# The last self-attention of a fused Perceiver kernel: V held in TensorE, the result not turned, one exponential per head, weighing a step later, division on POOL

## The chip, the cores and the metric

The kernel runs on one core of a Trainium2 chip, as one launch. The metric is device time in microseconds of a whole launch, from several runs. The trace shown is of one more execution, taken by the hardware profiler.

## What is computed

Two layers over 128 batches of 32 tokens of width 256 (`x`), each layer a cross-attention to 257 context rows, a self-attention and a feed-forward part. Only the last self-attention and what follows it are touched:

```python
x = x + _L1_attn_ref(_layernorm(x, axis=-1), L1_attn_W_qkv, L1_attn_W_out)
x = x + _L1_ffn_ref(_layernorm(x, axis=-1), L1_ffn_weight)

def _L1_attn_ref(x, W_qkv, W_out):        # 16 heads of 64, sequences of 32
    qkv = jnp.einsum('bse,ef->bsf', x, W_qkv)
    q, k, v = (qkv[:, :, 0], qkv[:, :, 1], qkv[:, :, 2])
    q = rotary_embedding(q, seq_len, HEAD_DIM)
    k = rotary_embedding(k, seq_len, HEAD_DIM)
    scores = jnp.einsum('bqhd,bkhd->bhqk', q, k) * scale
    scores = jnp.where(mask, scores, NEG_INF)          # causal
    weights = jax.nn.softmax(scores, axis=-1)
    out = jnp.einsum('bhqk,bkhd->bqhd', weights, v)
    return jnp.einsum('bsf,fe->bse', out, W_out)
```

`_L1_ffn_ref` is a BitLinear: a product with weights rounded to -1, 0, 1 and inputs rounded to 8 bits.

## The kernel before

The program runs stage after stage; the last, `SelfAttention1`, begins near 1975 us. It works in groups of 128 rows (4 batches of 32 tokens, `BPG` = 4), 32 groups. Work is pipelined over steps by hand: every engine's program walks through `steps()`, and in step g it does its share for group g (projections, rotation), for g - 1 (softmax), g - 2 (output projection) and, nine steps later, for the BitLinear. Engines wait for each other by named semaphores. What an engine does is in the order in which its function writes it.

In step g, TensorE (`tensor`) does: `project` of q and k in halves of 512 columns (each 6 matmuls, since every product is made of a high and a low part), between them `turn_out`, which turns the weighed and divided result of group g - 2 by eight transposes (L2243); `turn` of q's rotated halves (eight transposes, L2230); the `scores` of group g - 1 (L1161); v's first half; k's first turned half; `project_out` of g - 2 (24 matmuls); in one step of four, the next four groups' normalised input is turned (`ln.turn`, L353); k's second turned half; v's second half; the BitLinear's `turn` (L2122); `weigh` of group g - 1 (L1210); the BitLinear's `product` (L2139). Matrices in f32 of the scores and the weighing are recorded twice in the trace: 64 matmuls in the program are 128 there, and 32 are 64.

Results of the projections, of the turns, of the output projection and of the BitLinear share four PSUM banks (`Ring`): each use takes the next bank, and waits for the engine that emptied it four uses before. The scores lie in two banks of their own and the weighed result (`ps_out`) in two others.

VectorE (`vector`) forms the rotation's two products per half (`rotate`, L2365, L2368), the low part of the turned result (`attn_lo`, L2377), then the softmax of g - 1: mask and scale (L1181), maximum (L1186), shift (L1188), and, when ACT's one exponential of 512 columns (L1167) is done, the transpose in blocks of 32 (L1194), the sums (L1195) and their inverse (L1201); the addition of the output projection to X (L2403); statistics and rounding for other groups; the product of the weighed result with the inverse (L2424); the BitLinear's addition (L2146). POOL adds the rotation's two products (L2439) in two buffers `rot`, each of which it may overwrite when TensorE has turned it. ACT copies q, k (`keep_turned`, L2316), v (`keep_v`, L2309) and the high part of the turned result (`attn_hi`, L2323).

The weighing, which the change turns round, is

```python
ins = pe.do.matmul(out[rows, h, :], probT[rows, c0:c0 + T], v[rows, h * dv:(h + 1) * dv], start=True, stop=True)
```

with the turned probabilities (32 x 32) as the operand that is loaded and v (32 x 64) as the one that is streamed.

## Time and profile before

| | us |
|---|---|
| median of 3 runs | 2576.3 |
| lowest, highest | 2574.9, 2583.25 |
| the profiled execution | 2582.01 |
| its span, first to last instruction | 2580.1 |
| TensorE's mean granted clock in it | 0.964 of full |
| busy in the span: TensorE, its loads, VectorE, ACT, POOL | 2406.9, 1981.7, 1812.8, 1253.8, 841.0 |

A row of a timeline has the start, the duration, the engine, the line and the operation with its shape; several equal instructions in a row are merged, with their number behind x. Neighbours on an engine overlap, so what one costs is read from start to start. Rows of groups give the number, the total busy time and the mean duration in ns of one. Rows of windows give, for a stretch, its length, each engine's busy time with the number of instructions, TensorE's granted clock, and what the DMA engines did.

### The profile page before, as it was taken

The page shows a single profiled execution, that of the slowest core. Times are in us where ns is not written, and L with a number is a line of the kernel's source. Part 1 is how long each engine was busy: PE and PEld are TensorE (multiplying, and loading weights), DVE is VectorE, ACT ScalarE, POOL GpSimd, SP SyncE. Part 2 cuts the span into 40 slices and gives each one's busy share as a digit, 9 for nine tenths or more (in the row PEclk, how much of TensorE's full clock was granted, in tenths as well). Part 3 has the DMA queues.
Part 4 walks back from the last instruction along what each step waited for, and adds up shares of the span by engine and source line. Part 5 has one row for each costly group of instructions (what it writes and reads, how often), then busy time and mean ns, then how long its engine had stood idle before and what let it go on. Part 6 is the DMA issues. An engine that isn't in the chain of part 4 may idle for free. (4 is left out here: it accounts for less than half of the span.)

```text
span 2580.1 us, 103373 instructions
## 1 busy us (share of the span) xinstructions
PE 2406.9 (93%) x44640; PEld 1981.7 (77%) x44640; DVE 1812.8 (70%) x3820; ACT 1253.8 (49%) x2826; POOL 841.0 (33%) x740
## 2 busy tenths in 40 slices
PE   7999999999988867999996999999997999999997
PEld 6888888888855545888885777777776888888885
DVE  6778777777756664222225888888886788888886
ACT  5666666666544423333334777777763223232332
POOL 3333333332222112433335444444221333333231
PEclk9999999999998867999998999999997999999998
DMA  6555555554323244111115888887772000000000
GB/s 204 147 147 158 157 156 151 156 156 125 101 58 101 77 162 178 48 52 46 49 43 167 237 232 235 234 236 224 221 203 86 3 3 3 11 11 11 11 11 26
DMA packets 199554, 298.98 MB, mean 116 GB/s; under 512 B 29368, under 2 KB 107324, under 8 KB 197824
## 3 DMA queue, kind: packets, MB, share of 16 engines
q1 hardware_dynamic: 192288, 275.58, 36.1%
q0 software_dynamic: 6816, 16.79, 2.0%
q8 instruction: 356, 5.83, 1.0%
q14 instruction: 94, 0.77, 0.1%
HBM read 170.75 MB, written 78.77 MB: 97 GB/s over the span
## 5 line engine op out<-in xcount | busy, mean ns | idle before, releaser
L839 ACT ACTIVATE prob_x<-ps_score_x,neg_max_x 128x257 f32<-128x257 f32 x1024 | 403.6, 480 | 203.4 <-DVE neg_max_x L907 203.4
L907 DVE TENSOR_REDUCE neg_max_x<-ps_score_x 128x2 f32<-128x514 f32 x512 | 329.0, 684 | 108.2 <-PE ps_score_x L723 107.0
L734 PEld LDWEIGHTS ps_v_x<-v_wide_x,probT_x 128*32 128x32 f32 x18432 | 288.4, 108 | 126.8 <-issue 121.4
L734 PE MATMUL ps_v_x<-v_wide_x,probT_x 128*32 128x68 f32 x18432 | 336.0, 223 | 25.0 <-issue 20.2
L931 DVE STREAM_TRANSPOSE probT_x<-prob_x 128x1152 f32<-128x1152 f32 x256 | 344.0, 1344 | 0.0
L1073 POOL TENSOR_TENSOR ctxT_x_lo<-ready,ctxT_x_hi 128x514 fp32r<-128x514 f32 x128 | 153.0, 1196 | 386.5 <-ACT ctxT_x_hi L818 304.9
L2439 POOL TENSOR_TENSOR rot_s<-turned_s,swapped_s 128x512 f32<-128x512 f32 x128 | 164.5, 1297 | 327.7 <-DVE swapped_s L2368 288.1
L1073 POOL TENSOR_TENSOR split<-loaded,split 128x514 fp32r<-128x514 f32 x128 | 153.7, 1201 | 326.8 <-ACT split L818 302.2
L230 PE MATMUL ps_x<-split,w_q_x_hi 128*128 128x258 f32 x1024 | 208.0, 300 | 10.3 <-POOL split L1073 8.6
L1979 DVE TENSOR_TENSOR hid_moe<-ps_up_moe,silu_moe 128x512 f32<-128x512 f32 x71 | 49.1, 692 | 202.9 <-PE ps_up_moe L230 202.9
L723 PE MATMUL ps_score_x<-kT_x,q_x 32*64 32x257 f32 x4096 | 177.7, 401 | 14.3 <-ACT prob_x L839 10.3
L230 PEld LDWEIGHTS ps_x<-split,w_q_x_hi 128*128 128x128 f32 x1024 | 159.9, 192 | 31.0 <-issue 16.2
L830 ACT ACTIVATE kT_x<-ps_x,bias_k 128x257 f32<-128x257 f32 x256 | 122.2, 478 | 126.1 <-PE ps_x L230 125.6
L923 DVE STREAM_TRANSPOSE v_x<-ps_x 128x288 f32<-128x288 f32 x256 | 121.4, 480 | 74.3 <-PE ps_x L230 73.9
L230 PE MATMUL ps_x<-ctxT_x_hi,w_v_x_hi 128*128 128x258 f32 x512 | 159.0, 311 | 10.5 <-POOL ctxT_x_lo L1073 10.5
L230 PE MATMUL ps_x<-ctxT_x_hi,w_k_x_hi 128*128 128x258 f32 x512 | 146.4, 286 | 6.3 <-DVE v_x L923 6.3
L2323 ACT ACTIVATE attnT_s_hi<-ps_s 128x512 fp32r<-128x512 f32 x64 | 38.1, 599 | 231.4 <-PE ps_s L2243 231.4
L230 PE MATMUL ps_x<-split,w_q_x_lo 128*128 128x258 f32 x512 | 146.4, 286 | 0.5 <-issue 0.5
L230 PE MATMUL ps_x<-ctxT_x_lo,w_v_x_hi 128*128 128x258 f32 x512 | 145.0, 283 | 0.0
L230 PE MATMUL ps_x<-ctxT_x_hi,w_v_x_lo 128*128 128x258 f32 x512 | 144.9, 283 | 0.0
L230 PE MATMUL ps_x<-ctxT_x_lo,w_k_x_hi 128*128 128x258 f32 x512 | 144.9, 283 | 0.0
L230 PE MATMUL ps_x<-ctxT_x_hi,w_k_x_lo 128*128 128x258 f32 x512 | 144.4, 282 | 0.0
(296 smaller groups left out, 6010.0 us busy)
## 6 DMA issues: line engine op xcount, KB each, us to landing
v_wide_x<-v_x SPq DMA_DIRECT2D x512, 76.5 KB, 2.2
v_out_x<-v_x SPq DMA_DIRECT2D x128, 306.0 KB, 4.3
v_wide_x<-v_out_x SPq DMA_DIRECT2D x512, 76.5 KB, 3.1
ready<-ctx SPq DMA_DIRECT2D x128, 257.0 KB, 3.6
loaded<-ctx SPq DMA_DIRECT2D x128, 257.0 KB, 4.2
gate_whole<-moe_experts SPq DMA_DIRECT2D x32, 256.0 KB, 3.7
lo_out<-gate_whole SPq DMA_DIRECT2D x32, 256.0 KB
w_moe<-lo_out SPq DMA_DIRECT2D x8, 1024.0 KB, 8.3
```

The source lines that it names most:

```text
L230: last = pe.do.matmul(out, a, b, start=n == 0, stop=n == len(steps) - 1)
L723: ins = pe.do.matmul(self.ps[m * 2 * T:(m + 1) * 2 * T, r, 0:S], q, self.kT[b % 3][rows, m, 0:S], start=True, stop=True)
L734: ins = pe.do.matmul(self.ps_v[r * T:(r + 1) * T, b % 2, :, :], self.probT[b % 3][:, r, n * T:(n + 1) * T], self.v_wide[b % 4][:, :, r, n, ...
L830: act.do.activation(out, src, ACT.Identity, bias=self.biases["k"][:, m:m + 1]).then_inc(*s.k.at(tag, b, m))
L839: act.do.activation(self.prob[b % 3][:, r, 0:S], self.ps[:, r, 0:S], ACT.Exp, bias=self.neg_max[b % 2][:, r:r + 1]).then_inc(*s.exp.at(tag ...
L907: dve.do.tensor_reduce(self.neg_max[b % 2][:, r], self.ps[:, r, 0:S], AX_X, ALU.max, negate=True).then_inc(*s.neg_max.at(tag, b, half))
L923: dve.do.transpose(out.rearrange("p x n d -> p n x d"), src.rearrange("p (n x d) -> p n x d", x=2, d=XD)).then_inc(*s.v.at(tag, b, m))
L931: dve.do.transpose(flat(self.probT[b % 3]), flat(self.prob[b % 3])).then_inc(*s.prob_T.at(tag, b))
L1073: pool.do.tensor_tensor(self.ctxT[b % 3].lo[:, :, 0:S], self.ctx_in[g % 2][:, j, :, :], self.ctxT[b % 3].hi[:, :, 0:S].bitcast(F32), ALU.s ...
L1979: dve.do.tensor_tensor(self.hid[t % 2][:, :], self.up_ps[t % 2][:, :], self.silu[t % 2][:, :], ALU.mult).then_inc(*s.hid.at(t))
L2323: act.do.activation(self.attnT.hi[:, c * 512:(c + 1) * 512], banks["attn", g, c][:, :], ACT.Copy).then_inc(*s.a_hi.at(g, c))
L2439: pool.do.tensor_tensor(self.rot[e][:, :, :], self.turned[e][:, :, :], self.swapped[e][:, :, :], ALU.add).then_inc(*s.r_rot.at(g, i, c))
```

## The change

- The scores stand first in TensorE's step, and the weighing is that of group g - 2, behind the four half products of q and k. Scores and result now share four banks (`ps_halves`): scores in the first 256 columns of two, the result in the other 256 of all four. So the scores wait for the last use of the result (`a_lo`), and the weighing waits until VectorE has masked the new scores.
- In the weighing v is the operand that is loaded and the turned probabilities are streamed. The result then lies as the output projection needs it; `turn_out`, the tile `attn` and the semaphore `a_T` go.
- ACT takes one exponential per head, 16 of 32 columns, each with its maximum as bias and its sum as a second result. VectorE's shift and sums go. The inverse (`divide`) stays there.
- The probabilities are divided before they are weighed: POOL multiplies them with the inverse (`even`), behind its four rotation additions, and VectorE turns them after that. VectorE's product of the result with the inverse goes.
- On VectorE mask and maximum stand first in the step, the turn behind the other groups' statistics and rounding and ahead of the addition to X.

```diff
     def exponent(self, act, g):
+        s, t, e = self.s, self.t, g % 2
+        act.wait_ge(s.s_max, "s1", g)
         if g >= 2:
+            act.wait_ge(s.s_probT, "s1", g - 2)
+            act.wait_ge(s.s_inv, "s1", g - 2)
+        for n in range(H):
+            own = slice(n * T, (n + 1) * T)
+            ins = act.do.activation(t["prob"][e][:, own], t["shifted"][e][:, own], ACT.Exp, bias=t["neg_max"][e][:, n:n + 1],
+                                    accum_out=t["sums"][e][:, n:n + 1])
+        ins.then_inc(*s.s_exp.at("s1", g))
...
+    def even(self, pool, g):
+        s, t, e = self.s, self.t, g % 2
+        by_head = lambda a: a.rearrange("p (h q) -> p h q", q=T)
+        pool.wait_ge(s.s_inv, "s1", g)
+        pool.do.tensor_tensor(by_head(t["prob"][e][:, :]), by_head(t["prob"][e][:, :]),
+                              t["inv"][e][:, :].unsqueeze(2).to_broadcast([P, H, T]), ALU.mult).then_inc(*s.s_even.at(g))
+
+    def turn(self, dve, g):
+        s, t, e = self.s, self.t, g % 2
+        dve.wait_ge(s.s_even, g)
         if g >= 2:
-            dve.wait_ge(s.s_pv, tag, g - 2)
-        dve.do.transpose(t["probT"][e][:, :], t["prob"][e][:, :]).then_inc(*s.s_probT.at(tag, g))
...
+            dve.wait_ge(s.s_pv, "s1", g - 2)
+        dve.do.transpose(t["probT"][e][:, :], t["prob"][e][:, :]).then_inc(*s.s_probT.at("s1", g))
...
     def weigh(self, pe, g, out, v, dv):
-        s, tag, probT = self.s, self.tag, self.t["probT"][g % 2]
-        pe.wait_ge(s.s_probT, tag, g)
-        for h in range(H):
-            c0 = self.order.column[h]
-            for b in range(BPG):
-                rows = slice(b * T, (b + 1) * T)
-                ins = pe.do.matmul(out[rows, h, :], probT[rows, c0:c0 + T], v[rows, h * dv:(h + 1) * dv], start=True, stop=True)
-        ins.then_inc(*s.s_pv.at(tag, g))
+        s, probT = self.s, self.t["probT"][g % 2]
+        pe.wait_ge(s.s_probT, "s1", g)
+        for n in range(H // 2):
+            for x in range(2):
+                h = 2 * n + x
+                c0 = self.order.column[h]
+                for b in range(BPG):
+                    rows = slice(b * T, (b + 1) * T)
+                    ins = pe.do.matmul(out[x * dv:(x + 1) * dv, b, n, :], v[rows, h * dv:(h + 1) * dv], probT[rows, c0:c0 + T],
+                                       start=True, stop=True)
+        ins.then_inc(*s.s_pv.at("s1", g))
...
+    def out_part(self, c):
+
+        return self.out[:, 2 * c:2 * c + 2, :, :]
+
+    def attn_part(self, t, c):
+
+        return t[:, :].rearrange("p (n b q) -> p b n q", n=H // 2, q=T)[:, 2 * c:2 * c + 2, :, :]
```

TensorE's order within a step:

```diff
+            if before:
+                pe.wait_ge(s.r_qkT, g - 1, 1, self.NB - 1)
+                if g >= 3:
+                    pe.wait_ge(s.a_lo, g - 3, 0)
+                self.soft.scores(pe, g - 1, q_k)
             if now:
                 project(g, 0, 0)
                 project(g, 0, 1)
-            if out:
-                turn_out(g - 2, 0)
-            if now:
                 project(g, 1, 0)
                 project(g, 1, 1)
             if out:
-                turn_out(g - 2, 1)
+                pe.wait_ge(s.s_v, tag, g - 2, self.NB - 1)
+                if before:
+                    pe.wait_ge(s.s_masked, g - 1)
+                self.soft.weigh(pe, g - 2, self.out, self.v[g % 2], D1)
             if now:
+                project(g, 2, 0)
                 turn(g, 0, 0)
                 turn(g, 0, 1)
-            if before:
-                pe.wait_ge(s.r_qkT, g - 1, 1, self.NB - 1)
-                self.soft.scores(pe, g - 1, q_k)
-            if now:
-                project(g, 2, 0)
-                turn(g, 1, 0)
             if out:
                 project_out(g - 2)
+            if now:
+                turn(g, 1, 0)
             if n < SG and j == 3:
                 for k in range(KD):
                     self.ln.turn(pe, n, k, banks)
             if now:
                 turn(g, 1, 1)
-                project(g, 2, 1)
             if 0 <= last < G:
                 self.bit.turn(pe, last)
-            if before:
...
+            if now:
+                project(g, 2, 1)
             if 0 <= last < G:
                 self.bit.product(pe, last)
```

ACT's:

```diff
+            if before:
+                self.soft.exponent(act, g - 1)
             if out:
+                attn_hi(g - 2, 1)
                 attn_hi(g - 2, 0)
-                attn_hi(g - 2, 1)
             if now:
+                keep_v(g, 0)
                 keep_turned(g, 0, 0)
                 keep_turned(g, 0, 1)
```

VectorE's, and at the end POOL's:

```diff
+            if before:
+                self.soft.mask(dve, g - 1)
             if now:
                 rotate(g, 0, 0)
                 rotate(g, 0, 1)
             if g == 0:
                 self.wqkv[2].split_lo(dve)
-            if out:
-                attn_lo(g - 2, 0)
             if now:
                 rotate(g, 1, 0)
                 rotate(g, 1, 1)
+            if before:
+                self.soft.divide(dve, g - 1)
             if out:
                 attn_lo(g - 2, 1)
+                attn_lo(g - 2, 0)
+            if n < SG and j == 1:
+                for i in range(GPS):
+                    self.ln.take_stats(dve, n, i)
+            if n < SG and j == 2:
+                self.ln.scale(dve, n)
+            if 0 <= done < SG:
+                if jd == 1:
+                    self.bit.quantise(dve, done)
+                if jd == 2:
+                    self.bit.round_z(dve, done)
             if before:
-                self.soft.softmax(dve, g - 1)
+                self.soft.turn(dve, g - 1)
             if out:
                 dve.wait_ge(s.a_o_ps, g - 2)
                 dve.do.tensor_tensor(self.X[:, g - 2, :], self.X[:, g - 2, :], banks["o", g - 2][:, 0:D], ALU.add).then_inc(
                     *s.s_x1.at(g - 2))
             if n < SG and j == 3:
                 prepare(n)
-            if n < SG and j == 1:
-                for i in range(GPS):
-                    self.ln.take_stats(dve, n, i)
-            if n < SG and j == 2:
-                self.ln.scale(dve, n)
             if 0 <= g - 3 < G:
                 self.bit.take_stats(dve, g - 3)
-            if 0 <= done < SG:
-                if jd == 1:
-                    self.bit.quantise(dve, done)
-                if jd == 2:
-                    self.bit.round_z(dve, done)
-            if before:
-                dve.wait_ge(s.s_pv, tag, g - 1)
-                dve.wait_ge(s.s_inv, tag, g - 1)
-                if g >= 2:
-                    dve.wait_ge(s.a_T, g - 2, self.NB - 1)
-                dve.do.tensor_tensor(self.attn[:, :].rearrange("p (h d) -> p h d", d=D1), self.out,
-                                     self.t["inv"][(g - 1) % 2][:, :].unsqueeze(2).to_broadcast([P, H, D1]), ALU.mult).then_inc(
-                    *s.s_out.at(tag, g - 1))
...
+            if before:
+                self.soft.even(pool, g - 1)
```

What stands where is shown at two places. VectorE, the softmax and what follows it in one step before (`prob_s` are the probabilities, `X` the running sum):

```order
L1181 SCALAR_TENSOR_TENSOR shifted_s<-ps_score_s,constants 128x256 x2
L1186 TENSOR_REDUCE neg_max_s<-shifted_s 128x16
L1188 TENSOR_TENSOR shifted_s<-shifted_s,neg_max_s 128x512
L1194 STREAM_TRANSPOSE probT_s<-prob_s 128x512
L1195 TENSOR_REDUCE sums_s<-prob_s 128x16
L1201 RECIPROCAL inv_s<-sums_s 128x2x8
L2403 TENSOR_TENSOR X<-X,ps_s 128x256
```

And in the change, from the inverse to the next group's maximum, in a step that also rounds for the BitLinear:

```order
L1188 RECIPROCAL inv_s<-sums_s 128x16
L2375 TENSOR_TENSOR attnT_s_lo<-ps_halves_s,attnT_s_hi 128x2x8x32 x2
L2113 TENSOR_SCALAR xn_bit<-xn_bit,inv_bit 128x256 x4
L2116 TENSOR_SCALAR xn_bit<-xn_bit 128x1024
L2118 TENSOR_SCALAR xn_bit<-xn_bit 128x1024
L1202 STREAM_TRANSPOSE probT_s<-prob_s 128x512
L2414 TENSOR_TENSOR X<-X,ps_s 128x256
L2076 BN_STATS stats_bit<-X 128x6
L2078 BN_AGGR mv_bit<-stats_bit 128x2
L2150 SCALAR_TENSOR_TENSOR X<-ps_s,back_bit,X 128x256
L1166 SCALAR_TENSOR_TENSOR shifted_s<-ps_halves_s,constants 128x256 x2
L1170 TENSOR_REDUCE neg_max_s<-shifted_s 128x16
```

The transpose of the probabilities, which followed the shift at once, now stands behind the other groups' rounding and directly ahead of the addition to X; the mask and the maximum of the next group end the row, at the head of the next step.

POOL in the last stage had only the rotation's additions, with a root now and then. In the change, around two steps (`rot_s` are the rotated halves, `rstd` and `var` the norms' statistics):

```order
L1194 TENSOR_TENSOR prob_s<-prob_s,inv_s 128x512
L2432 TENSOR_TENSOR rot_s<-turned_s,swapped_s 128x512 x4
L1194 TENSOR_TENSOR prob_s<-prob_s,inv_s 128x512
L321 TENSOR_TENSOR ln_rstd_s<-ln_var_s,constants 128x4
L2432 TENSOR_TENSOR rot_s<-turned_s,swapped_s 128x512 x4
```

The division (L1194) of a group stands behind all four additions of the step.

## Rows read from the trace of the kernel before

**Rows 1.** Busy time by stretch: the last stage's opening, and its steady part

```profile
1975.00:1999.00 24.00, 21.59 (x332) 17.32 (x331) 15.01 (x34) 8.25 (x13) 8.06 (x7) 0.81 0.01 2
2141.00:2529.00 388.00, 384.66 (x7304) 334.50 (x7303) 322.26 (x703) 117.05 (x223) 120.32 (x97) 1.00 0.03 9
```

**Rows 2.** Timeline of TensorE, step 2: the scores of group 1

```profile
2006.47 1.29 PE L1161 MATMUL ps_score_s<-loaded 64*32 64x32 f32 x128
```

**Rows 3.** Timeline of TensorE, one whole step, 2501.84 to 2521.60 us

```profile
2501.84 1.99 PE L1210 MATMUL ps_out_s<-loaded,probT_s 32*32 32x64 f32 x128
2503.76 0.39 PE L2139 MATMUL ps_s<-wq_bit,zT_bit 128*128 128x256 bf16 x2
2503.91 0.71 PE L230 MATMUL ps_s<-split,xT_s_hi 128*128 128x512 f32 x2
...
2506.75 0.60 PE L2243 MATMUL ps_s<-constants,attn_s 128*128 128x128 f32 x4
2507.10 0.48 PE L230 MATMUL ps_s<-w_qkv_s_hi,xT_s_hi 128*128 128x512 f32 x1
...
2509.98 0.60 PE L2243 MATMUL ps_s<-constants,attn_s 128*128 128x128 f32 x4
2510.42 1.04 PE L2230 MATMUL ps_s<-constants,rot_s 128*128 128x128 f32 x8
2511.39 1.29 PE L1161 MATMUL ps_score_s<-loaded 64*32 64x32 f32 x128
2512.60 0.50 PE L230 MATMUL ps_s<-w_qkv_s_hi,xT_s_hi 128*128 128x512 f32 x1
...
2514.11 0.60 PE L2230 MATMUL ps_s<-constants,rot_s 128*128 128x128 f32 x4
2514.46 0.36 PE L230 MATMUL ps_s<-w_out_s_hi,attnT_s_hi 128*128 128x256 f32 x1
...
2517.39 0.60 PE L2230 MATMUL ps_s<-constants,rot_s 128*128 128x128 f32 x4
...
2521.60 0.71 PE L230 MATMUL ps_s<-split,xT_s_hi 128*128 128x512 f32 x2
```

**Rows 4.** TensorE, first self-attention's scores and what follows; loads of two forms (min/median/max ns)

```profile
868.90 0.86 PE L1332 MATMUL ps_score_s<-kT_s,q_s 32*64 32x32 f32 x64
869.69 0.55 PE L353 MATMUL ps_s<-constants,ln_xn_moe 128*128 128x128 f32 x3
...
L1332 PEld LDWEIGHTS ps_score_s<-kT_s,q_s x2048: 127/131/227, 743.1 to 934.3; 32*64 32x64 f32 x187
...
L1210 PEld LDWEIGHTS ps_out_s<-loaded,probT_s x4096: 101/105/105, 1996.4 to 2548.5; 32*32 32x32 f32 x196
```

**Rows 5.** Groups of POOL, whole program

```profile
L2439 POOL TENSOR_TENSOR rot_s<-turned_s,swapped_s 128x512 f32<-128x512 f32 x128 | 164.5, 1297 | 327.7 <-DVE swapped_s L2368 288.1 <-PE ps_s L2230 37.7
...
L1082 POOL TENSOR_TENSOR loaded<-loaded,share_routed 128x1024 f32<-128x1024 f32 x14 | 26.5, 1895 | 0.0
```

**Rows 6.** Groups of VectorE, last stage; and its timeline, the shift

```profile
L2377 DVE TENSOR_TENSOR attnT_s_lo<-ps_s,attnT_s_hi 128x512 fp32r<-128x512 f32 x64 | 43.4, 681 | 2.1 <-ACT attnT_s_hi L2323 2.1
...
L1194 DVE STREAM_TRANSPOSE probT_s<-prob_s 128x512 f32<-128x512 f32 x32 | 22.8, 713 | 22.3 <-ACT prob_s L1167 22.3
...
L2403 DVE TENSOR_TENSOR X<-X,ps_s 128x256 f32<-128x256 f32 x32 | 13.4, 419 | 19.0 <-PE ps_s L230 19.0
...
2514.23 0.69 DVE L1188 TENSOR_TENSOR shifted_s<-shifted_s,neg_max_s 128x512 f32<-128x512 f32 x1
```

**Rows 7.** Groups of ACT, whole program; and its timeline, four exponentials

```profile
L839 ACT ACTIVATE prob_x<-ps_score_x,neg_max_x 128x257 f32<-128x257 f32 x1024 | 403.6, 480 | 203.4 <-DVE neg_max_x L907 203.4
...
L1167 ACT ACTIVATE prob_s<-shifted_s 128x512 f32<-128x512 f32 x32 | 20.2, 632 | 92.4 <-DVE shifted_s L1188 92.4
...
L1448 ACT ACTIVATE prob_moe<-logit_moe 128x32 f32<-128x32 f32 x8 | 1.8, 229 | 10.4 <-DVE logit_moe L1456 10.3
...
1502.86 1.58 ACT L839 ACTIVATE prob_x<-ps_score_x,neg_max_x 128x257 f32<-128x257 f32 x4 [0.99 <-DVE neg_max_x L907]
```

110 lines of the change are left out of this document (36 added, 74 removed).

## The prediction

> **What bounds the kernel now.** Read the busy time by stretch first [rows 1]: in the steady part of the last stage TensorE is busy for 384.66 of 388.00 us at the full clock (1.00, the 2.4 GHz level), while VectorE has 83% (322.26 of 388), ACT 30%, POOL 31%. So what TensorE issues is the bound there; only the opening (21.59 busy of 24) and the tail are bound by chains. Then one step in order of time [rows 3], from 2503.91 to 2521.60: 17.69 us. Each piece's cost is the distance to the next piece's start, since the durations overlap. The scores of group 1 start at 2006.47 [rows 2] and those of group 29 at 2511.39 [rows 3], 28 steps of 18.03 us on average, so this one is 0.34 under the mean. Everything before 1975 us is the same program before and after.
>
> **The change, part by part.** Steps are counted from the moment at which TensorE starts a piece [rows 3].
>
> (1) The eight transposes of the weighed result (L2243) go: 2507.10 - 2506.75 = 0.35 and 2510.42 - 2509.98 = 0.44 us.
>
> (2) The weighing takes 2503.76 - 2501.84 = 1.92 us for 128 recorded matmuls, 15.0 ns each, with 32 columns loaded and 64 streamed. It becomes 64 loaded and 32 streamed. The trace has exactly that form in the first self-attention's scores (32*64, 32x32) [rows 4]: 64 of them in 869.69 - 868.90 = 0.79 us, 12.3 ns each, so 128 x 12.3 = 1.58 us, 0.34 less. The ends: the pace of the last self-attention's own scores, 2512.60 - 2511.39 = 1.21 us for 128, and no gain at all, 1.92. I take 1.58, the row of the same form. The Trainium skill ("TensorE: Matmul & The Clock Gate", section on LDWEIGHTS) says that a load's time goes with its columns; by that the new order, with twice the columns to load, would be slower, not faster. The rows of the loads agree in kind, 131 ns against 105 [rows 4], but the pace of the pair is what TensorE pays, and that is lower in the row. The rule has a rival below.
>
> (3) The rest of TensorE's step is moved, not changed. With the starts of rows 3 I lay it out anew, in us from the start of the scores: scores 0 (1.21 long), q's and k's four half products 1.21 to 6.96 (1.51 + 1.44 after the scores, 2.80 for the next two, which no longer follow transposes), weighing 6.96 to 8.54, v's first half to 10.05 (1.51), q's eight transposes to 10.85 (0.35 + 0.45), output projection to 13.78 (2.93 = 2517.39 - 2514.46), k's eight transposes to 14.58, then 0.31 for the BitLinear's two, v's second half from 14.89 to 16.37 and the BitLinear's product to 16.52 (0.15 = 2503.91 - 2503.76; the 0.31 and 1.48 are what is left of 2521.60 - 2517.39 without 0.36 for four transposes, 1.92 and 0.15, shared as two transposes and six matmuls go elsewhere in the step). So 17.69 - 16.52 = **1.17 us less per step**, if nothing makes TensorE wait.
>
> (4) POOL's division is a new link. POOL has only two rotation buffers, so its third addition waits until TensorE has turned the first: that was at once done before, and is now behind the weighing. q's first transposes start at 10.05 and end at 10.65 (0.60 long [rows 3]). Then two additions (1.30 long [rows 5], and I take 1.25 from one to the next) put the division at 13.19. What does it cost? An addition of 512 columns on POOL took 1.30, a product with a broadcast operand of 1024 columns 1.90 [rows 5]; half of the latter is 0.95. I take 1.30, the row of the same size; the ends are 0.95 and 1.90. It ends at 14.49. VectorE, held there, then turns the probabilities (0.71 long) and adds to X (0.42) [rows 6], the second starting 0.08 before the first ends, as neighbours on VectorE do: 14.53, 15.16, 15.58. v's second half takes the bank that this addition to X empties (four banks in a ring: output, k's two, the BitLinear's turn, v) and would start at 14.89. So **TensorE waits 15.62 - 14.89 = 0.73 us** in each step that has a BitLinear turn in it (from step 9 on). The three or four tasks that stand ahead of the turn on VectorE end earlier in most steps. The earlier steps have no such turn; there v's second half takes another bank, and the wait is absent.
>
> (5) Sixteen exponentials per group instead of one. Their length: 480 ns for 257 columns with a bias from memory, four in 1.58 us, so 367 ns apart; one column costs (632 - 229) / 480 = 0.84 ns [rows 7]. For 32 columns that is 291 ns long and 178 apart: 16 x 0.178 = 2.9 us. No row shows an activation that also writes its sum. If the sum is free it is 2.9 us; if each sum is an instruction of its own as long as the 32-column activation (229 ns) and nothing overlaps, 16 x (291 + 229) = 8.3 us. They start where the shift started, 2514.23 - 2511.39 = 2.84 after the scores' start [rows 3, 6]. ACT then makes two copies of the weighed result (0.63 each at most, by the 512-column activation [rows 7]) and VectorE two subtractions (0.68 each [rows 6]) behind them, each of these 0.04 to 0.08 less from start to start: the copies can start at 8.65, when the weighing's last result is out, the last subtraction is ready at some 10.6, and the output projection wants it at 10.85. From 2.84 to 8.65 are 5.8 us, and 0.2 more are slack, so there is room for 6.0 us of exponentials before anyone waits. The middle of the two ends, 5.6, is still hidden, so I put this at nothing. The cover is ACT's idle time, 70% of the stretch [rows 1]; were it gone, the 5.6 would show in every step.
>
> (6) VectorE loses the shift (0.69 [rows 6]), the sums and the product with the inverse; at 83% it isn't the bound, so this buys only room. Reading the result in four banks and writing it in runs of 32 I put at the old rows' durations.
>
> (7) **Opening and tail.** In the opening the weighing of group 0 (1.92) leaves its step, and some of the 2.41 us idle [rows 1] can be filled: 3 us less, ends 0 and 5. The tail, 2580.1 - 2521.60 = 58.5 us now, loses the transposes and gains the exponentials and the division in its two chains: 1 us less, ends -6 and +4.
>
> The sum: eight early steps 8 x 1.17 = 9.4; 21 late ones 21 x (1.17 - 0.73) = 9.2; the mean of a step is 0.34 above 17.69, over 29 steps 10 us, most of it the normalised groups' transposes, which stay; of its gaps I let 2.1 go, ends 0 and 4; opening and tail 4. Together 24.7. The profiled execution took 2582.0 us (span 2580.1) and would take 2557.3; the median of the runs is 5.7 us lower, 2576.3, so I forecast **2551 us**.
>
> **The rivals.**
>
> A. The sums hold up ACT. At 8.3 us the exponentials end 2.3 us past the 6.0 that are free. The output projection starts that much later, the 0.73 is swallowed by it, and a late step takes 16.52 + 2.3 = 18.8 against 17.69, an early one as much more than now. That is 1.1 in 29 steps, 32 us, and some 5 in the tail, less 3 of the opening: 2610 us, slower. It decides from 6.0 + 1.17 = 7.2 us of exponentials, 450 ns each. For: no row shows the form. Against: it needs no overlap at all, where neighbours overlap by 113 ns each [rows 7]. The Trainium skill ("VectorE: DVE Perf Modes", section on two Vector instructions with no wait between them) says that an operation that writes its accumulator out is two instructions; if ACT does the same, this rival is how it would hurt. No row here shows it.
>
> B. The division is slow on POOL, 1.9 us. Then the wait is 1.33, a late step saves nothing (-0.16), and what is left is 9.4 + 2.1 + 4 - 3.4 = 12: 2564 us.
>
> C. Loading bounds the weighing. Then it goes with the loads' rows, 1.92 x 131 / 105 = 2.40 us, 0.82 more than my term in 31 groups, 25 us: 2576 us, no change. Against it stands the pace of the same form [rows 4].
>
> D. Better than forecast: weighing at the scores' pace, 1.21 (0.37 x 31 = 11), and a division of 1.05 (0.25 x 21 = 5): 2535 us.
>
> **How the numbers follow.** Forecast 0.50, A 0.10, B 0.15, C 0.06, D 0.19. The predicted time is the forecast's. The range runs from just below D (the opening's end too) to above B: 2532 to 2572 us; outside lie A, most of C and the lower part of D. A measurement can tell 0.3% (7.7 us) from no change. Faster: forecast, B and D less a little of B that ends near 2569, 0.82. Same: C and that part, 0.08. Slower: A, 0.10.
>
> **What would show it.** In the changed profile: no L2243 transposes; the weighing (ps_halves) at about 1.6 us from start to start; a late step of some 17.2 us between scores; TensorE idle before v's second half, released by VectorE's addition to X, 0.7 us per step; POOL's division near 1.3 us, waiting for nothing on POOL itself but standing behind two additions that waited for TensorE's transposes; the exponentials of a group within 6 us. It is wrong if a late step takes 17.7 or more, if the output projection waits for the rest of the result (A), if the weighing's pace is above 15 ns (C), or if the step is 16.6 with no wait at all (then the link in (4) isn't there).

## The result and the profile after

The changed kernel takes **2592.03 us** (median of 10 runs, 2584.77 to 2599.34) against 2582.06 for the kernel before (median of 10, 2574.9 to 2587.06; the 2576.3 of the start was the median of its first three, so 5.8 us of what my forecast missed lie in its starting point). The ratio is 1.0032, 95% interval 1.002 to 1.0043: slower, by a little more than the 0.3% that I said a measurement can tell. I forecast 2551 us. The profiled execution took 2592.01 us (span 2590.2), against 2582.01 (2580.1) before.

Busy time by stretch, after; the rows answer to [rows 1] (columns: stretch, its length, busy us and instructions of TensorE, its loads, VectorE, ACT and POOL, granted clock, DMA share, GB/s).

```profile
1975.00:1999.00 24.00, 18.19 (x205) 13.93 (x206) 15.80 (x36) 12.63 (x45) 8.99 (x8) 0.93 0.01 2
2141.00:2529.00 388.00, 359.15 (x7087) 301.75 (x7086) 305.66 (x621) 205.04 (x858) 138.91 (x114) 0.98 0.03 9
```

TensorE was busy for 384.66 of the 388 us before and is for 359.15 now, at a clock of 0.98: it has less to do, and waits. VectorE is busy for 305.66 us where it was for 322.26, though the change took away three of its instructions in every step.

One late step on TensorE, from one group's scores to the next, answers to [rows 3]: 2471.03 to 2490.59, 19.56 us.

```profile
2471.03 1.29 PE L1157 MATMUL ps_halves_s<-loaded 64*32 64x32 f32 x128
...
2478.02 1.49 PE L1213 MATMUL ps_halves_s<-probT_s,loaded 32*64 32x32 f32 x128
2479.44 0.50 PE L230 MATMUL ps_s<-w_qkv_s_hi,xT_s_hi 128*128 128x512 f32 x1
...
2480.94 1.03 PE L2240 MATMUL ps_s<-constants,rot_s 128*128 128x128 f32 x8
...
2484.66 1.03 PE L2240 MATMUL ps_s<-constants,rot_s 128*128 128x128 f32 x8
2485.53 0.38 PE L2126 MATMUL ps_s<-constants,xn_bit 128*128 128x128 f32 x2
2487.95 0.50 PE L230 MATMUL ps_s<-w_qkv_s_hi,xT_s_hi 128*128 128x512 f32 x1 [2.04 <-DVE X L2414]
...
2490.01 0.65 PE L2143 MATMUL ps_s<-wq_bit,zT_bit 128*128 128x256 bf16 x2
```

Up to 2485.53 the step is shorter than I laid it out (the BitLinear's turn starts 14.50 us in; I had 14.58). Then v's second half waits for VectorE's addition to X: the view shows 2.04 us of idle time, and it starts 16.92 us in, where I had 15.62 after a wait of 0.73. The waits of TensorE in the steady stretch, in sum (us, times, longest):

```profile
PE ps_s L230 <- DVE X L2414: 15.9, 16, 2.1
PE ps_s L2240 <- DVE X L2414: 11.2, 5, 2.2
```

The second row is the same wait in the five steps that also turn the layer norm's input: there k's second turned half takes the bank that the addition to X empties.

What holds VectorE is in the timelines of VectorE and POOL of the same step:

```profile
2480.24 1.29 DVE L2375 TENSOR_TENSOR attnT_s_lo<-ps_halves_s,attnT_s_hi 128x512 fp32r<-128x512 f32 x2 [0.52 <-ACT attnT_s_hi L2322]
2481.45 4.06 DVE L2113 TENSOR_SCALAR xn_bit<-xn_bit,inv_bit 128x256 f32<-128x256 f32 x4
2485.55 0.69 DVE L2116 TENSOR_SCALAR xn_bit<-xn_bit 128x1024 f32<-128x1024 f32 x1
2486.27 0.69 DVE L2118 TENSOR_SCALAR xn_bit<-xn_bit 128x1024 f32<-128x1024 f32 x1
2486.88 0.71 DVE L1202 STREAM_TRANSPOSE probT_s<-prob_s 128x512 f32<-128x512 f32 x1
2487.51 0.38 DVE L2414 TENSOR_TENSOR X<-X,ps_s 128x256 f32<-128x256 f32 x1
```

```profile
2475.43 2.68 POOL L2432 TENSOR_TENSOR rot_s<-turned_s,swapped_s 128x512 f32<-128x512 f32 x2 [9.82 <-DVE swapped_s L2367]
2481.71 2.59 POOL L2432 TENSOR_TENSOR rot_s<-turned_s,swapped_s 128x512 f32<-128x512 f32 x2 [3.60 <-PE ps_s L2240]
2484.26 1.10 POOL L1194 TENSOR_TENSOR prob_s<-prob_s,inv_s 128x512 f32<-128x512 f32 x1
```

Four TENSOR_SCALARs of 256 columns take 4.06 us. They start 0.26 before POOL's two additions and its division, and end 0.15 after them; the first of 1024 columns, next to no POOL instruction, takes its usual 0.69. Taken one by one, the first of the four takes 0.345 us and the others end at 2483.155, 2484.452 and 2485.511, each 0.15 behind the end of a POOL instruction (2483.004, 2484.300, 2485.360). Lengths over the stage (min/median/max ns), after and then before:

```profile
L2097 DVE TENSOR_SCALAR xn_bit<-X,mv_bit,rstd_bit x24: 403/1256/1391, 2091.8 to 2464.6; 128x256 f32<-128x256 f32 x24
L2113 DVE TENSOR_SCALAR xn_bit<-xn_bit,inv_bit x24: 343/1258/1454, 2112.2 to 2484.4; 128x256 f32<-128x256 f32 x24
L333 DVE TENSOR_SCALAR ln_xn_s<-X,ln_mean_var_s,ln_rstd_s x28: 404/1256/1394, 2010.5 to 2447.3; 128x256 f32<-128x256 f32 x28
```

```profile
L2093 DVE TENSOR_SCALAR xn_bit<-X,mv_bit,rstd_bit x24: 382/407/412, 2103.2 to 2467.2; 128x256 f32<-128x256 f32 x24
L2109 DVE TENSOR_SCALAR xn_bit<-xn_bit,inv_bit x24: 321/347/350, 2120.3 to 2483.8; 128x256 f32<-128x256 f32 x24
```

So three of every four are held up, in all three tasks: the BitLinear's quantising (L2097) and rounding (L2113) and the layer norm's scaling (L333). They do not cost the same. Late steps without a task take 17.1 to 17.5 us; those that round 18.7 to 20.2; those that quantise 19.7 to 21.3, of which some 1.6 are the layer norm's transposes that fall into the same step (18.03 against 16.44 in run 4 below). A late step that only scales takes 17.3, or 18.3 where TensorE also waits 0.85 ahead of the scores, as it does in run 4. Its four end at 2448.49, 0.15 behind POOL's division, and the turn that waits for the division follows at once (VectorE's timeline):

```profile
2444.42 4.07 DVE L333 TENSOR_SCALAR ln_xn_s<-X,ln_mean_var_s,ln_rstd_s 128x256 f32<-128x256 f32 x4
2448.41 0.70 DVE L1202 STREAM_TRANSPOSE probT_s<-prob_s 128x512 f32<-128x512 f32 x1
```

Behind the rounding's four stand two passes of 0.69, behind the quantising's a maximum of 1.22 and three short instructions; these are what the held-up task pushes past the division. Early steps take 16.0 us, with the scaling or with no task (17.36 before).

For the experiments one measure is used beside the time: the start of group 29's scores less that of group 1's, 28 steps, as for [rows 2, 3]. Before: 2511.39 - 2006.47 = 504.92. Seven of the 28 are early and 21 late, so by my terms it should have come to 504.92 - 8.2 - 9.2 - 2.1 = 485.4. After: 2508.04 - 2000.06 = 507.98. It is read from one profiled execution each, which lies within 4 us of the median; only that of run 4 is lower, the fastest of its five (2543.44 us, median 2550.04).

### The profile page after: what moved, and what is told of

The parts are those of the page before. It is cut to its first block and busy times, and to the rows that moved or that the text cites. A ratio compares the mean times of both kernels' runs of the same rounds, so it can differ in the third digit from the quotient of the medians.

```text
span 2590.2 us, 103714 instructions
## 1 busy us (share of the span) xinstructions
PE 2375.4 (92%) x44384; PEld 1940.6 (75%) x44384; DVE 1791.9 (69%) x3724; ACT 1392.5 (54%) x3818; POOL 874.8 (34%) x772
## 5 line engine op out<-in xcount | busy, mean ns | idle before, releaser
L1181 ACT ACTIVATE prob_s<-shifted_s,neg_max_s 128x32 f32<-128x32 f32 x512 | 156.7, 308 | 80.4 <-DVE neg_max_s L1170 80.4
```

Source lines behind the costliest of these rows:

```text
L1181: ins = act.do.activation(t["prob"][e][:, own], t["shifted"][e][:, own], ACT.Exp, bias=t["neg_max"][e][:, n:n + 1], accum_out=t["sums"][e] ...
```

## The experiments

Theory **T1**: POOL's instructions hold up VectorE's TENSOR_SCALARs out of and into SBUF, and the change made them meet. Rivals: **T2**, the place of the tasks ahead of the turn and the addition to X is what costs, held up or not; **T3**, the link through POOL's two buffers and the division alone; **T4**, ACT's exponentials and their sums.

**1. Tasks behind the addition to X** (`e1_tasks_behind`).

```diff
-            if n < SG and j == 1:
-                for i in range(GPS):
-                    self.ln.take_stats(dve, n, i)
...
             if before:
                 self.soft.turn(dve, g - 1)
...
                 self.bit.take_stats(dve, g - 3)
+            if n < SG and j == 1:
+                for i in range(GPS):
+                    self.ln.take_stats(dve, n, i)
+            if n < SG and j == 2:
+                self.ln.scale(dve, n)
+            if 0 <= done < SG:
+                if jd == 1:
+                    self.bit.quantise(dve, done)
+                if jd == 2:
+                    self.bit.round_z(dve, done)
```

> The changed kernel, but VectorE does its tasks (the sums and the scaling of the MLP's layer norm, the BitLinear's quantising and rounding) behind the turn of the probabilities and the addition to X, no longer ahead of them. Theory T1 (the tasks' TENSOR_SCALARs of 256 columns lose time because POOL computes at that moment, some 1100 ns instead of 400, and with them ahead the turn and the addition to X come late): they now run when POOL's additions and its division are over, take about 400 ns again, and the steps of 18.7 to 21.3 us fall to about 17.3; 55 us of VectorE's time go, of which I expect 30 to 45 in the result: 2550 to 2565 us against 2592. Rival T2 (their place ahead of the addition delays, whether stretched or not): the same gain, but the TENSOR_SCALARs may stay long. Rival T3 (the division's link alone, behind POOL's two rotation buffers): the link stays, steps stay, 2592 +- 5. Rival T4 (ACT's exponentials and their sums): 2592 +- 5.

Measured: 2562.1 us, ratio to before 0.9931 (0.9909 to 0.9952). The 28 steps take 484.42 us. The quantising's lengths (min/median/max ns):

```profile
L2097 DVE TENSOR_SCALAR xn_bit<-X,mv_bit,rstd_bit x28: 382/408/411, 2095.9 to 2514.4; 128x256 f32<-128x256 f32 x28
```

The timeline of VectorE with a rounding and the next step's turn, and that of TensorE with the wait that is left:

```profile
2462.01 1.11 DVE L2113 TENSOR_SCALAR xn_bit<-xn_bit,inv_bit 128x256 f32<-128x256 f32 x4
...
2477.68 0.71 DVE L1202 STREAM_TRANSPOSE probT_s<-prob_s 128x512 f32<-128x512 f32 x1 [3.75 <-POOL prob_s L1194]
```

```profile
2478.75 0.50 PE L230 MATMUL ps_s<-w_qkv_s_hi,xT_s_hi 128*128 128x512 f32 x1 [0.45 <-DVE X L2404]
```

What follows: the tasks cost 30 us, and without them ahead the 28 steps take what the prediction summed (484.42 against 485.4), with plain late steps of 17.15 us. The whole is still 11 us above the forecast's 2551: 5.8 of it are the starting point, and the 4 us that I took from opening and tail are not seen (outside the 28 steps 2074.9 us against 2075.2 before). T3 and T4 as the cause of the loss fall; T1 and T2 stand, since lengths and place changed together.

**2. Division on VectorE** (`e2_div_on_vector`).

```diff
             if before:
+                self.soft.even(dve, g - 1)
                 self.soft.turn(dve, g - 1)
...
-            if before:
-                self.soft.even(pool, g - 1)
```

> The changed kernel with the division of the probabilities by their sums on VectorE, right ahead of the turn, instead of on POOL. Order of the tasks kept. T3 (link through POOL's buffers and division): the link is cut, the turn no longer waits for POOL, and 0.5 to 1.5 us go from each of 31 steps: 2550 to 2575. T1: the TENSOR_SCALARs still run beside POOL's last two additions and still lose most of it (mean 900 ns instead of 1050), VectorE gets 31 x 0.7 us more work: 2575 to 2592, with the long steps still at 18.5 us or more. T2: as T1, with unchanged lengths. T4: 2592.

Measured: 2588.92 us, ratio 1.0024 (1.0009 to 1.004); 28 steps 510.37. POOL now has two additions beside the tasks instead of three instructions, and four TENSOR_SCALARs take 3.34 us instead of 4.06 (groups of VectorE, steady stretch):

```profile
L2097 DVE TENSOR_SCALAR xn_bit<-X,mv_bit,rstd_bit 128x256 f32<-128x256 f32 x20 | 16.7, 893 | 0.0
L2113 DVE TENSOR_SCALAR xn_bit<-xn_bit,inv_bit 128x256 f32<-128x256 f32 x20 | 16.4, 878 | 0.0
```

The time lies in the upper part of T1's range and outside that of T3 (2550 to 2575), whose link is cut here. The division's place is not the trouble.

This run also shows that the delay goes both ways. Where VectorE's division, which reads two tensors from SBUF, had begun 0.27 us before one of POOL's additions, that addition took 1.57 us instead of 1.30 (three times; min/median/max of POOL's additions):

```profile
L2433 POOL TENSOR_TENSOR rot_s<-turned_s,swapped_s x120: 1281/1299/1572, 1999.0 to 2533.0; 128x512 f32<-128x512 f32 x120
```

**3. Another instruction for the same work** (`e3_one_port`), for the quantising, shown, and the layer norm's scaling alike.

```diff
-            ins = dve.do.tensor_scalar(xn[:, j, :], self.X[:, g, :], self.mv[:, g, 0:1], self.rstd[:, g:g + 1], ALU.subtract, ALU.mult)
+            ins = dve.do.scalar_tensor_tensor(out=xn[:, j, :], in0=self.X[:, g, :], scalar=self.mv[:, g, 0:1],
+                                              in1=self.rstd[:, g:g + 1].to_broadcast([P, D]), op0=ALU.subtract, op1=ALU.mult)
```

> The changed kernel with its order untouched, but the layer norm's scaling and the BitLinear's quantising are computed with another instruction of the same size and result, a SCALAR_TENSOR_TENSOR with the scale broadcast as its second tensor. The rounding's first pass stays a TENSOR_SCALAR, as the control. T1, if only the form TENSOR_SCALAR is held up by POOL: the replaced ones take some 400 ns each and no longer 990 to 1080, the rounding's stay at about 900, and 37 us of VectorE's time go: 2565 to 2575. T2 (order alone): their length changes nothing much, 2585 to 2595. T3, T4: 2592. If the new form is held up too, or is slow by itself (800 ns), the run decides nothing by its time, only by its lengths.

Measured: 2594.85 us, ratio 1.004 (1.0019 to 1.0061); 28 steps 511.19. A miss: the form is held up too.

```profile
L334 DVE SCALAR_TENSOR_TENSOR ln_xn_s<-X,ln_mean_var_s,ln_rstd_s x28: 475/1388/1524, 2011.2 to 2451.8; 128x256 f32<-128x256 f32 x28
```

Its shortest is 475 ns, so it isn't slow by itself. It reads two tensors from SBUF. VectorE's STREAM_TRANSPOSE (711 ns beside POOL, 703 apart), its statistics (394 against 417) and the rotation's products, which read PSUM (415 and 692 ns either way), kept their lengths; its maximum over the scores never ran beside POOL here. The time decides nothing, as said before the run. The Trainium skill has the rule that I missed ("SBUF — State Buffer", section "SBUF: two separate sides"): VectorE and POOL share a pair of SBUF ports under an exclusive lock that is held for a whole instruction, taken by VectorE where it runs in a two-port mode or, against a POOL instruction that reads SBUF, where it reads two inputs from SBUF; whichever starts first has it. Both forms of this run agree with it, at 1258 and 1388 ns where 344 and 475 are the shortest, and so does POOL's addition in run 2. That the lock is always held for a whole instruction the trace of run 1 does not bear out. POOL's root there (a TENSOR_TENSOR of four columns, usually 1.02 us) started inside the first of four scaling TENSOR_SCALARs and took 0.23 longer, but the other three ran beside it at 408 to 412 ns, not held up:

```profile
2146.02 1.38 DVE L333 TENSOR_SCALAR ln_xn_s<-X,ln_mean_var_s,ln_rstd_s 128x256 f32<-128x256 f32 x4
2146.19 1.25 POOL L2087 TENSOR_TENSOR rstd_bit<-var_bit,constants 128x4 f32<-128x4 f32 x1 [1.88 <-DVE var_bit L2082]
```

**4. Four rotation buffers** (`e4_rot4`).

```diff
-        self.rot = [sb(f"rot{i}", [P, self.HB, D1]) for i in range(2)]
+        self.rot = [sb(f"rot{i}", [P, self.HB, D1]) for i in range(4)]
...
-            if old:
-                pool.wait_ge(s.r_T, *old)
-            pool.do.tensor_tensor(self.rot[e][:, :, :], self.turned[e][:, :, :], self.swapped[e][:, :, :], ALU.add).then_inc(
+            if g:
+                pool.wait_ge(s.r_T, g - 1, i, c)
+            pool.do.tensor_tensor(self.rot[i * 2 + c][:, :, :], self.turned[e][:, :, :], self.swapped[e][:, :, :], ALU.add).then_inc(
```

> The changed kernel with four rotation buffers instead of two, so that POOL's third and fourth additions no longer wait for TensorE's transposes, which the change put behind the weighing; nothing else moved. POOL then adds at once and its division waits only for the exponentials' sums. T1: POOL's work moves away from VectorE's tasks in part; where it does, the TENSOR_SCALARs are short again and the long steps fall to 17.3; 2545 to 2570. T3: the 0.4 to 0.7 us in front of v's second half go in every late step, but the tasks stay as long as they are: 2575 to 2585. T2: the addition to X still stands behind the tasks: 2585 to 2592. T4: 2592.

Measured: **2550.04 us, ratio 0.9877 (0.9852 to 0.9901)**, the fastest kernel here. 28 steps take 471.06; a plain late step takes 16.44. POOL's second pair of additions starts 7.3 us into the step (scores at 2466.42) instead of 10.7, and VectorE's tasks, still ahead of the turn and the addition to X, are short again but for one in four, 0.70 us beside the end of the division (POOL's timeline; one line of VectorE):

```profile
2473.72 2.66 POOL L2432 TENSOR_TENSOR rot_s<-turned_s,swapped_s 128x512 f32<-128x512 f32 x2 [0.23 <-DVE swapped_s L2367]
```

```profile
L2097 DVE TENSOR_SCALAR xn_bit<-X,mv_bit,rstd_bit x32: 399/403/715, 2086.5 to 2526.6; 128x256 f32<-128x256 f32 x32
```

In TensorE's list of waits the addition to X is no longer named. So T2 falls: the tasks' place was kept and the long steps are gone. One buffer size removes both the meeting and the link.

**5. Both together** (`e5_rot4_behind`): the edits of 1 and 4.

> Four rotation buffers and VectorE's tasks behind the addition to X, both in one. The four buffers alone gave late steps of 16.44 us (18.03 in those with the layer norm's transposes) and 2550 us. If the lock by POOL (T1) and the link through POOL's buffers (T3) are all that was lost, nothing is left for the moved tasks: 2550 +- 4. If the tasks' place costs something by itself (T2): 2535 to 2545. If tasks behind the addition now come late for the BitLinear: 2555 or more.

Measured: 2552.93 us, ratio 0.9878 (0.9857 to 0.9898), 28 steps 476.56; plain late steps 16.44. Nothing is left for the tasks' place, again against T2.

**6. POOL busy in the kernel before** (`e6_before_filler`).

```diff
+            if 2 <= g < G + 2:
+                pool.wait_ge(s.s_x1, g - 2)
+                for i in range(3):
+                    if g > 2 or i:
+                        pool.wait_ge(s.r_rot, g - 2 - (i == 0), "filled", i - 1 if i else 2)
+                    pool.do.tensor_tensor(self.spare[:, :], self.consts["ones"][:, 0:1].to_broadcast([P, 512]),
+                                          self.consts["ones"][:, 0:1].to_broadcast([P, 512]), ALU.add).then_inc(
+                        *s.r_rot.at(g - 2, "filled", i))
```

> The kernel before, with three additions of 512 columns added on POOL in each step, into a tile that nobody reads, started when VectorE has added to X, so that POOL computes while VectorE does its tasks; everything else as in the kernel before. T1 (POOL's instructions hold up VectorE's TENSOR_SCALARs out of and into SBUF): these go from 405 and 342 ns to 900 ns or more, and those that read PSUM, the sums and the reductions stay; since nothing waits closely for VectorE's tasks in the order of before, the time moves by 0 to 40 us. T2, T3: the lengths stay at 405 and 342 ns.

Measured: 2598.18 us, ratio 1.0058 (1.0035 to 1.0081), 28 steps 514.66. The scaling (L335) and the rounding (L2111) of the kernel that never had the trouble now have it:

```profile
L335 DVE TENSOR_SCALAR ln_xn_s<-X,ln_mean_var_s,ln_rstd_s x28: 406/1161/1197, 2011.6 to 2455.5; 128x256 f32<-128x256 f32 x28
...
L2111 DVE TENSOR_SCALAR xn_bit<-xn_bit,inv_bit x24: 340/998/1196, 2119.8 to 2493.6; 128x256 f32<-128x256 f32 x24
```

The quantising, which starts later behind the same addition, reached a mean of only 559 ns, less than I expected. The order of before pays 10 us for it in the 28 steps and 15 in the whole, less than the changed kernel does; that nothing there waits closely for the tasks is the likely reason, and was not tested.

**7. POOL busy, nothing else** (`e7_rot4_filler`): kernel 4 with the three additions of run 6, released by the last subtraction ahead of the tasks:

```diff
+                pool.wait_ge(s.a_lo, g - 2, 0)
```

> The changed kernel with four rotation buffers, and three additions of 512 columns added on POOL in each step, into a tile that nobody reads, started when VectorE's last subtraction ahead of its tasks is done. VectorE's order, TensorE's order and all waits are those of the run with four buffers (2550 us). T1: the TENSOR_SCALARs go back from 420 to 480 ns to some 1100, the steps that have them grow from 16.44 to 18.5 or more, and the time goes back to 2575 to 2595, though no link was put back. T3 (only the link through the buffers mattered): 2550 +- 5. T2: 2550 +- 5.

Measured: 2581.89 us, ratio 0.9991 (0.9972 to 1.0009), 28 steps 503.58. Four TENSOR_SCALARs beside three additions:

```profile
2475.50 3.98 DVE L2115 TENSOR_SCALAR xn_bit<-xn_bit,inv_bit 128x256 f32<-128x256 f32 x4
```

```profile
2476.00 3.32 POOL L2450 TENSOR_TENSOR spare_s<-constants 128x512 f32<-128x512 f32 x3
```

This is the run that separates T1 from T3: buffers, waits and orders are those of run 4, POOL alone has more to do, and 32 us come back, within the range that T1 gave. The additions cost nothing where no task meets them: plain late steps take 16.4 to 16.8 us, as in run 4. Steps that quantise or round take 18.7 to 21.2; those that scale from 17.2, less than the 18.5 that I expected of all three.

**8. Exponentials twice** (`e8_exp_twice`), on kernel 4; the additional sixteen go into a tile nobody reads.

```diff
+        for n in range(16):
+            own = slice(n * T, (n + 1) * T)
+            act.do.activation(t["again"][e][:, own], t["shifted"][e][:, own], ACT.Exp, bias=t["neg_max"][e][:, n:n + 1],
+                              accum_out=t["sums_again"][e][:, n:n + 1])
```

> The changed kernel with four rotation buffers, and each of the sixteen exponentials of a group done twice, first into a tile that nobody reads. ACT's exponentials of a group took 5.0 us from first to last in the changed kernel; now 9.9. If there is room for 6.0 us, as the prediction has it, each step grows by 3.9 us at most, the output projection waiting for the copies of the weighed result: 31 x 3.9 = 121, 2670 us; if there is more room than that because the copies could start later, less, down to 2550. If ACT's work is on the path already (T4), all of the 4.9 us show: 2700 us.

Measured: 2729.93 us, ratio 1.0565 (1.0536 to 1.0593); the 28 steps take 632.7, 22.6 each. More than any theory had. The output projection waits 3.77 us (TensorE's timeline; the view names no releaser, but it starts 0.1 behind VectorE's last subtraction), which is about what I gave, but then it runs at half the clock (windows of it: 24 matmuls, 0.50):

```profile
2582.32 0.55 PE L230 MATMUL ps_s<-w_out_s_hi,attnT_s_hi 128*128 128x256 f32 x1 [3.77 <-issue]
```

```profile
2568.00:2577.00 9.00, 9.00 (x252) 7.48 (x251) 7.09 (x16) 6.62 (x44) 4.59 (x4) 1.00 0.03 7
2577.00:2582.00 5.00, 1.55 (x11) 1.12 (x9) 1.32 (x3) 5.00 (x27) 1.63 (x2) 0.91 0.00 0
2582.30:2587.50 5.20, 5.18 (x24) 5.20 (x25) 3.51 (x9) 0.45 (x1) 0.00 (x0) 0.50 0.00 0
```

The projection takes some 5.2 us instead of the 2.93 of [rows 3], 2.3 more for a wait of 3.8. The fall does not follow every such wait. Two of the 28 steps, those from 2319.1 and 2592.1, wait as long, keep the clock at 1.00 and take 20.41 and 20.42 us: 3.97 and 3.98 more than the 16.44 of run 4, against 3.9 expected. So the wait's size agrees with the prediction's room, and what comes on top is the clock.

**9. Twenty exponentials** (`e9_exp_20`): the same edit with `range(4)`.

> The changed kernel with four rotation buffers, and four of the sixteen exponentials of a group done twice, so twenty pairs instead of sixteen: 6.2 us from first to last instead of 5.0. In the run with four buffers ACT sits idle for 0.67 us between the last exponential and the copies of the weighed result, so the copies come 0.55 us later. If the room is the prediction's 6.0 us plus nothing, 0.2 to 0.5 us per step show, 6 to 15 us in all: 2556 to 2565; a step of 16.6 to 16.9. If the room is 7 us or more: 2550 and 16.44. If TensorE's clock falls after each such wait, as it did with the doubled exponentials (0.50 in the stretch behind a wait of 3.8 us), 1 us or more per step: 2580.

Measured: 2555.38 us, ratio 0.99 (0.9866 to 0.9934). A plain late step takes 16.78, 0.34 more than in kernel 4; 28 steps take 480.95, 9.9 more. The step is as expected, the time just under its range (2556 to 2565). The four pairs are 1.2 us, so 0.9 of them are hidden: there is room for sixteen pairs and about three more. TensorE's clock stayed at 1.00 in all 28 steps.

**10. POOL writes only** (`e10_rot4_memset`): run 7 with memsets of 1024 columns.

```diff
+                    pool.do.memset(self.spare[:, :], 1.0).then_inc(*s.r_rot.at(g - 2, "filled", i))
```

> The run with four rotation buffers and the three additional POOL additions, but with three POOL memsets of 1024 columns in place of the additions: POOL writes to SBUF and reads nothing there. If any POOL instruction holds up VectorE's TENSOR_SCALARs, those of 256 columns take 600 ns or more and the time is 2560 to 2590; if only POOL instructions that read SBUF do, they take 410 to 480 ns and it is 2550 +- 5.

Measured: 2579.81 us, ratio 0.9993 (0.9977 to 1.0008), 28 steps 504.03.

```profile
L335 DVE TENSOR_SCALAR ln_xn_s<-X,ln_mean_var_s,ln_rstd_s 128x256 f32<-128x256 f32 x28 | 28.1, 1063 | 0.0
```

So it is POOL's instruction, whether or not it reads SBUF, that holds up the TENSOR_SCALAR. The same section of the Trainium skill's page says that VectorE's instructions with two SBUF inputs are spared beside a POOL instruction that only writes; no run here shows that part.

| kernel | us | 28 steps | tasks held up |
|---|---|---|---|
| before | 2582.06 | 504.92 | no |
| changed | 2592.03 | 507.98 | yes |
| 1: tasks behind | 2562.1 | 484.42 | no |
| 4: four buffers | 2550.04 | 471.06 | one in four, in part |
| 7: four buffers, POOL adds | 2581.89 | 503.58 | yes |
| 10: four buffers, POOL writes | 2579.81 | 504.03 | yes |

## Why the prediction was wrong

(1) and (2), the transposes and the weighing: right, a little better than forecast. The weighing costs 2479.44 - 2478.02 = 1.42 us; I had 1.58, between the ends 1.21 and 1.92. Early steps lost 1.38 us (17.36 to 15.98) where I had 1.17. Rival C, that the loads bound the weighing, is out: the loads take 131 ns where they took 105 [rows 4], and the pair is faster all the same. The rule of the Trainium skill weighed in (2) ("TensorE: Matmul & The Clock Gate", section on LDWEIGHTS) so agrees in kind for the load and does not give the pace of the pair.

(3) The new layout: right. Without any wait a late step takes 16.44 us (run 4); I had 16.52.

(4) The link through POOL: right in kind, and in size in part by luck. POOL's third addition waits for TensorE's transposes (3.60 us idle), the division takes 1.05 to 1.10 us where I took 1.30 between 0.95 and 1.90 (rival B is out), and the step costs 17.15 - 16.44 = 0.71 with the link and nothing else (runs 1 and 4); I had 0.73. Two errors of one size cancel there: v's second half starts at 15.33 with the link (I had 15.62), the division being cheaper, and at 14.63 without it (I had 14.89). **The step that failed is the sentence behind it: "The three or four tasks that stand ahead of the turn on VectorE end earlier in most steps."** It puts the tasks' part in the wait at nothing. It holds in the six late steps that have no task. In the five that scale the tasks end 0.15 us behind the division, and in the ten that quantise or round far behind it. Taken at the lengths of before they would not: the rounding starts 10.42 us after the scores (2481.45 - 2471.03) and would take 1.11 + 1.38 us (run 1: 4 in 1.11; two of 0.69), to 12.9, ahead of the division's end at 14.33; the quantising would end near 13.5 (10.40 + 1.4 + 1.7). The rounding took 4.06 + 1.38, and the turn started at 15.85. I took the lengths from a trace in which POOL was idle at that time, and moved POOL's work onto it with the very argument of (4). One event starts both: the weighing's end lets ACT and VectorE take the result out, behind which the tasks come, and lets TensorE turn q, which frees POOL's buffers 0.26 us later.

What it cost: 507.98 - 484.42 = 23.6 us over the 28 steps, and 3.4 in the tail (from group 29's scores to the end 82.2 us, in run 1 78.8). In the step shown the price is an idle time of 2.04 us in place of 0.45 (run 1), and behind it TensorE at half its clock:

```profile
2471.03:2485.90 14.87, 14.87 (x329) 12.91 (x328) 13.12 (x24) 8.72 (x40) 6.25 (x5) 1.00 0.01 4
2487.95:2490.00 2.05, 2.05 (x6) 1.31 (x6) 0.46 (x2) 0.00 (x0) 0.00 (x0) 0.70 0.00 0
2490.00:2492.00 2.00, 2.00 (x131) 1.59 (x130) 0.48 (x1) 0.60 (x1) 0.00 (x0) 0.50 0.00 0
2492.00:2495.00 3.00, 3.00 (x28) 2.43 (x15) 2.64 (x6) 1.31 (x9) 0.00 (x0) 0.97 0.46 180
```

19.56 - 16.44 = 3.12 us for the step: v's second half starts 2.28 later than in run 4 (16.92 against 14.64), and what follows takes 0.84 more at the lower clock, which no term of mine had. The clock does not fall each time. Another step that rounds, with the same wait, kept it and took 0.83 less (windows of whole steps):

```profile
2397.16:2415.89 18.73, 16.68 (x338) 14.06 (x337) 15.60 (x29) 9.62 (x42) 6.25 (x5) 1.00 0.01 2
2471.03:2490.59 19.56, 17.52 (x338) 14.40 (x337) 15.60 (x29) 9.82 (x42) 6.25 (x5) 0.95 0.01 3
```

Of the eleven waits of 2.04 to 2.25 us in the 28 steps, six were followed by such a fall. The five late ones cost 0.8 to 1.6 us in their step and up to 0.35 in the next, against steps of the same kind at full clock: some 7 of the 23.6 us, by my estimate. No run took this part away alone.

(5) The exponentials: hidden, as forecast. They are pairs, an ACTIVATE and an ACTIVATION_READ_ACCUMULATOR, 0.31 us from pair to pair and 5.0 for sixteen; I had bounds of 2.9 and 8.3 and the middle, 5.6.

```profile
2473.87 0.32 ACT L1181 ACTIVATE prob_s<-shifted_s,neg_max_s 128x32 f32<-128x32 f32 x1 [2.37 <-DVE neg_max_s L1170]
2474.10 0.19 ACT L1181 ACTIVATION_READ_ACCUMULATOR prob_s<-shifted_s,neg_max_s 128x1 f32 x1
2474.19 0.31 ACT L1181 ACTIVATE prob_s<-shifted_s,neg_max_s 128x32 f32<-128x32 f32 x1
...
2479.54 1.08 ACT L2322 ACTIVATE attnT_s_hi<-ps_halves_s 128x512 fp32r<-128x512 f32 x2 [0.69 <-PE ps_halves_s L1213]
```

ACT is idle for 0.69 us behind them. Four more pairs (run 9) are 1.2 us and cost 0.34, so 0.9 are free and the room is 5.9; I had 6.0. Here the forecast's ground was a guess between two bounds, and the bounds were far apart (2.9 and 8.3): that it fell on the right side of 6.0 was in part luck. Rival A had the second instruction right and its price wrong: pairs overlap. What the Trainium skill states of it for VectorE ("VectorE: DVE Perf Modes", section on two Vector instructions with no wait between them) these rows show for ACT.

(6) VectorE has less to do, but waits for POOL inside its own instructions, and the profile counts that as busy: 305.66 us of the steady stretch, against 287.59 in kernel 4, which does the same work and gets through more steps in it.

(7) Opening and tail: not confirmed. Outside the 28 steps run 4 takes 2541.6 - 471.06 = 2070.5 us against 2075.2 before, 4.7 less, where I had 4; but run 1 takes 2074.9 and run 5 2075.5, and the changed kernel itself 2082.2. The start of group 0's scores varied between 1977.9 and 1985.7 among the runs on the changed kernel, whose opening is the same, so terms of 3 us there can't be judged.

No rival had the mechanism. The sum of the terms was right for a kernel in which VectorE's tasks keep their lengths: 485.4 forecast for the 28 steps, 484.42 in run 1.

## What to carry to other kernels

When work moves onto POOL or moves in time there, list VectorE's fp32 TENSOR_SCALARs between SBUF tiles and its instructions with two SBUF inputs that then fall beside it, and price each at one POOL instruction more (here 407 to 1256 ns in the median), not at the length it had while POOL was idle. Then ask what stands behind them: the scaling was held up as long as the rounding, but cost a late step 0.14 us (17.28 against 17.14), for it ended with the POOL work that the next instruction waited for anyway. A busy share doesn't show this: compare the mean duration of the same instruction in both traces. A second pair of buffers that lets POOL run early can be worth more than the arithmetic removed: it took the changed kernel from 2592 to 2550 us. Whether it would help the kernel before was not run.

## What the runs showed of the hardware

- Four TENSOR_SCALARs beside three POOL instructions last as long as these three and 0.4 to 0.7 us more (4.06 against 3.65 from 2481.71 to 2485.36 in the changed kernel, 3.98 against 3.32 in run 7), as if the two engines took turns instruction by instruction: each held one ends 0.15 us behind a POOL instruction. POOL's own additions stay at 1.3 us beside them (a pair in 2.59, 2.68 where VectorE's are not held).
- POOL is delayed too, where VectorE's instruction began first: an addition took 1.57 us instead of 1.30 beside VectorE's division (run 2), its root of four columns 1.25 instead of 1.02 beside a TENSOR_SCALAR (run 1). That root held up none of the TENSOR_SCALARs that followed (406 to 412 ns).
- A POOL memset, which reads nothing, holds them up as an addition does (1063 ns mean).
- A wait of TensorE can have a second price. Behind 2.04 us of idle time the granted clock was 0.70 and then 0.50 (1.2 GHz) for some 4 us; behind 3.77 us it was 0.50 for the 5.2 us of the output projection. It is not sure to come: behind five of eleven waits of 2.04 to 2.25 us in the changed kernel, and behind two of those of some 3.8 in run 8, the clock stayed at 1.00. It stayed there behind every wait of up to 1.2 us in the steady stretches of runs 1, 4 and 9.
- An activation that also writes its sum is two instructions on ACT, 0.31 and 0.19 us long, 0.31 from pair to pair.
